# Two cross-attention layers on one core: L0's keys written once to DRAM, and each batch's rows loaded in four transfers

## The reference, cut to what matters

```
q = x @ Wq + bq          # 32 query heads of 16
k = ctx @ Wk + bk        # 8 key heads of 16, each shared by 4 query heads
v = ctx @ Wv + bv
attn = softmax(q k^T / 4 + mask)
x = layernorm((attn v) @ Wo + bo + x)
```

## Time and profile before

| | |
|---|---|
| median of 3 runs | 2464.18 us |
| profiled execution | 2464.88 us, its span 2463.0 us |
| granted TensorE clock, mean | 0.981 |
| moved by DMA | 250.46 MB in 134533 packets |
| SyncE's queue (q1) | 90863 packets, 125.37 MB, 17.0% of 16 engines |
| ScalarE's queue (q10) | 43496 packets, 122.76 MB, 16.2% |

### The profile page before, as it was taken

The page is one execution under the profiler, slowest core; times in us unless marked ns, Lnnn a source line. Parts: engine busy times, 40 slices in busy tenths (PEclk is TensorE's granted clock), DMA queues, the critical chain, the costliest instruction groups (busy, mean ns, idle before and its releaser), DMA issues. The chain is left out here.

```text
span 2463.0 us, 36589 instructions
## 1 busy us (share of the span) xinstructions
PE 2320.6 (94%) x13464; PEld 2087.0 (85%) x13464; DVE 1401.3 (57%) x3146; ACT 999.3 (41%) x2195; POOL 765.6 (31%) x823
## 2 busy tenths in 40 slices
PE   6898899999999999998988979999999999999998
PEld 5666899998989999997876769998989999998976
DVE  4687645454565455456548965455546655454574
ACT  3685433243433333243238944243334333243420
POOL 2132322415141423313531331414141422415055
PEclk9899999999999999999999989999999999999999
DMA  8351323233323323234363213333332323233222
GB/s 279 96 156 39 92 85 108 87 91 116 99 86 96 95 82 111 82 96 146 125 198 96 77 40 95 97 101 97 103 95 82 96 90 107 86 87 121 79 76 79
DMA packets 134533, 250.46 MB, mean 102 GB/s; under 512 B 31151, under 2 KB 54831, under 8 KB 133335
## 3 DMA queue, kind: packets, MB, share of 16 engines
q1 hardware_dynamic: 90863, 125.37, 17.0%
q10 hardware_dynamic: 43496, 122.76, 16.2%
HBM read 223.19 MB, written 29.48 MB: 103 GB/s over the span
## 5 line engine op out<-in xcount | busy, mean ns | idle before, releaser
L674 POOL TENSOR_SCALAR wk_hi<-raw 128x512 fp32r<-128x512 f32 (+1 forms) x84 | 54.0, 643 | 905.5 <-DMA raw<-in_wk 747.5
L1411 ACT ACTIVATE probs<-scores,prm 112x376 f32<-112x376 f32 x256 | 147.1, 575 | 342.9 <-DVE prm L1805 342.8
L794 PE MATMUL pj_two<-ctx_hi,wk_hi 128*128 128x376 f32 x708 | 243.6, 344 | 7.7 <-DVE rr L1566 4.1
L1566 DVE TENSOR_TENSOR rr<-pj_two,rr 128x448 fp32r<-128x448 f32 (+2 forms) x223 | 147.0, 661 | 172.6 <-ACT rr L1177 172.2
L795 PE MATMUL pj_two<-ctx_lo,wk_hi 128*128 128x376 f32 x708 | 239.0, 338 | 0.0
L796 PE MATMUL pj_two<-ctx_hi,wk_lo 128*128 128x376 f32 x708 | 238.5, 337 | 0.0
L794 PE MATMUL pj_two<-pt_hi,nat 125*128 125x448 f32 x531 | 198.8, 374 | 10.6 <-issue 10.2
L676 POOL TENSOR_TENSOR wb_lo<-raw,wb_hi 128x512 fp32r<-128x512 f32 x152 | 197.9, 1302 | 12.7
L1568 DVE SCALAR_TENSOR_TENSOR k_lo<-pj_two,cur,k_hi 128x375 fp32r<-128x375 f32 x167 | 101.3, 607 | 173.1 <-ACT k_hi L1179 172.6
L796 PE MATMUL pj_two<-pt_hi,nat 125*128 125x448 f32 x531 | 195.4, 368 | 0.0
L795 PE MATMUL pj_two<-pt_lo,nat 125*128 125x448 f32 x531 | 195.2, 368 | 0.0
(11 more groups left out here) (278 smaller groups left out, 6611.1 us busy)
## 6 DMA issues: line engine op xcount, KB each, us to landing
nat<-nat_scratch ACTq DMA_DIRECT2D x256, 384.0 KB, 3.7
raw<-in_wq SPq DMA_DIRECT2D x72, 256.0 KB, 3.3
raw<-in_wo SPq DMA_DIRECT2D x72, 256.0 KB, 2.6
raw<-in_wk SPq DMA_DIRECT2D x64, 256.0 KB, 3.8
raw<-in_wv SPq DMA_DIRECT2D x64, 256.0 KB, 4.2
raw<-in_w SPq DMA_DIRECT2D x64, 256.0 KB, 2.9
nat_scratch<-rr ACTq DMA_DIRECT2D x7, 1536.0 KB, 8.8
k_hi<-keys_scratch SPq DMA_DIRECT2D x32, 188.0 KB, 2.8
```

What stands on the lines that cost most here:

```text
L674: nc.gpsimd.tensor_scalar(hi, src, 1.0, 0.0, ALU.mult, ALU.add).then_inc(split_hi, 1)
L794: nc.tensor.matmul(dst, l_hi, r_hi, start=first, stop=False)
L1411: nc.scalar.activation(probs[0:L, h, 0:SK], scores[n % SCR][0:L, 0:SK], ACT.Exp, bias=neg_max[0:L, h:h + 1], accum_out=row_sum[0:L, h:h + ...
L1566: i = nc.vector.tensor_tensor(dst, src, hi.bitcast(F32), ALU.subtract)
```

## The change

The scratch loses its dimension e, so keys are stored once: two transfers a batch in place of four. The second copy is made by the load, which reads each 16 rows twice, by a source whose first dimension has step 0 and count 2. This needs one transfer for each key head and part: four of 32 rows in place of one of 128. The semaphore counts follow.

```diff
--- before.py
+++ after.py
@@ -254,7 +254,7 @@
 
     ctx_dram = nc.dram_tensor("ctx_copy", (D, HB, S), F32, kind="Internal").ap()
 
-    k_dram = nc.dram_tensor("keys0_scratch", (HALVES, HB, 8, 2, 2, HD0, SK), F32, kind="Internal").ap()
+    k_dram = nc.dram_tensor("keys0_scratch", (HALVES, HB, 8, 2, HD0, SK), F32, kind="Internal").ap()
     q_dram = nc.dram_tensor("queries0_scratch", (HALVES, C0, HPC, 2, HD0, T), F32, kind="Internal").ap()
 
     x_dram = nc.dram_tensor("x_copy", (D, B * L), F32, kind="Internal").ap()
@@ -433,21 +433,23 @@
                     load_rows(base + RAW_A + ag * RAW_GU, wk, ag // G1 * D, ag % G1 * GW)
 
                 def store_keys0(b, split, n):
-
                     sp.wait_ge(split, n)
                     for r in range(2):
-                        for e in range(2):
-                            sp.dma_start(k_dram[hf, b, :, r, e, :, :], k0_split[b % 2][r].bitcast(F32)).then_inc(k0_out[b % 2], 16)
+                        sp.dma_start(k_dram[hf, b, :, r, :, :], k0_split[b % 2][r].bitcast(F32)).then_inc(k0_out[b % 2], 16)
 
                 def load_keys0(c, b):
+
                     if c == 0:
-                        sp.wait_ge(k0_out[b % 2], (hf * 2 + b // 2 + 1) * 64)
+                        sp.wait_ge(k0_out[b % 2], (hf * 2 + b // 2 + 1) * 32)
                     else:
 
                         sp.wait_ge(sc_ready, hf * SC_H + (c - 1) * HB * HPC + (b + 1) * HPC)
                     sp.sem_inc(sp_passed, 1)
-                    sp.dma_start(k_hi[:, b, :].bitcast(F32),
-                                 k_dram[hf, b, 2 * c:2 * c + 2].rearrange("g r e d n -> (g r e d) n")).then_inc(k0_in[b], 16)
+                    for kv in range(KV2):
+                        for r in range(2):
+                            at = 64 * kv + 32 * r
+                            sp.dma_start(k_hi[at:at + 32, b, :].bitcast(F32),
+                                         k_dram[hf, b, 2 * c + kv, r].unsqueeze(0).broadcast_to([2, HD0, SK])).then_inc(k0_in[b], 16)
 
                 def store_queries0(c, split, n):
                     sp.wait_ge(split, n)
@@ -921,7 +923,7 @@
                 def scores0(n):
                     c, b, j = n // (HB * HPC), n // HPC % HB, n % HPC
                     if n % HPC == 0:
-                        pe.wait_ge(k0_in[b], (hf * C0 + c + 1) * 16)
+                        pe.wait_ge(k0_in[b], (hf * C0 + c + 1) * 64)
                         if c > 0:
                             pe.wait_ge(q0_in[b], (hf * (C0 - 1) + c) * 64)
                         elif b == 0:
@@ -1292,7 +1294,7 @@
                 def keys0(b, bank, ready, n, mid):
 
                     if hf * 2 + b // 2 > 0:
-                        act.wait_ge(k0_out[b % 2], (hf * 2 + b // 2) * 64)
+                        act.wait_ge(k0_out[b % 2], (hf * 2 + b // 2) * 32)
                     if hf == 0 and b == 0:
                         act.wait_ge(setup_dve, 1)
                     move(k0_split[b % 2][0], bank[:, 0:SK], ready, n, bias=bk0, mid=mid)
@@ -1364,7 +1366,7 @@
                         exps0(n + 3)
                     if n == 20:
                         for t in k0_out:
-                            act.wait_ge(t, (hf + 1) * 2 * 64)
+                            act.wait_ge(t, (hf + 1) * 2 * 32)
                         act.sem_inc(w_free["k"], 1)
                     if n >= 16 and n % 8 == 0:
                         out0((n - 16) // 8)
```

## The result

| | before | after |
|---|---|---|
| median | 2464.72 us (2457.64 to 2472.16, 20 runs) | 2469.14 us (2466.25 to 2472.86, 20 runs) |
| ratio of after to before, 95% interval | | 1.0018 [1.0011, 1.0024] |
| profiled execution, its span | 2464.88, 2463.0 us | 2467.31, 2465.5 us |
| granted clock, mean | 0.981 | 0.981 |

The changed kernel is 4.4 us slower (2.7 to 5.9 by the interval). A second set of 7 runs gave 2469.61 us against 2464.27, ratio 1.0029 [1.0018, 1.0040]: 5.3 us by the medians, 4.4 to 9.9 by the interval. The sign and the range held. The size did not: I had 12.

A forecast was written before the change was run, and what follows sets the result against it. TensorE, busy 94% of the span, was taken as the bound, so only its waits in L0 count. Terms 1.0 + 5.4 + 3.8 + 1.0 + 1.0 = +12.2 us gave 2476 us, range 2463 to 2487.

The forecast's parts named there:

- (a): Half 0 until the queries of c = 0 land: three store batches -6.6, loads of two batches +7.6, sum +1.0 us.
- (b): From queries landed to ScalarE's eviction into pt_hi: loads of batches 2 and 3 +3.8 each, batch 3's stores -2.2, sum +5.4 us.
- (c): Half 0, c = 2, batch 0: 56 more rows on the engine pair delay the load and queries behind by +3.8 us.
- (e): TensorE's longer waits keep the clock low longer: one more low stretch, about +1 us, bounds 0 and +3.
- (d): Half 1 until its last query store lands: three store batches -6.6, loads of batches 0 and 1 +7.6, sum +1.0 us.
- saved stores win: Rival: loads spread over sixteen engines or land early enough, so only the stores' saving counts; 2451 us, chance 0.10.
- They cancel: Rival: engine pairs rotate, or the pair was not late before 59.90 us; +2 us, 2466 us, chance 0.13.
- Late weights too: Rival: in c = 2 weight loads behind four key loads reach GpSimd late, 5 to 10 us more; 2484 us, chance 0.07.
- some query weights reach GpSimd sooner: Sign that the forecast is wrong: query weights reaching GpSimd sooner than before the change.
- landing of key loads: Sign: key loads land after some 6 us and more where they were 2.8; 3 us would be wrong.

The follow-up runs named there:

- loads alone: Keys stored twice as in the kernel before, but loaded by four transfers of 32 rows with the repeat: 2485.97 us, 1.0095 of the kernel before.
- stores alone: Keys stored once, loaded by one transfer of 128 successive rows (partly wrong keys): 2446.32 us, 0.9935 of the kernel before.
- again: The changed kernel, same code, run and profiled a second time: 2469.61 us, 1.0029 of the kernel before.
- eight loads of 16 rows: Changed kernel with each 32-row load split into two of 16 rows without the repeat, eight a batch: 2462.91 us, 0.9996 of the kernel before.
- pair only for c = 0: Changed kernel with repeating loads only for c = 0, one 128-row load (partly wrong keys) for c = 1 to 3: 2468.41 us, 1.0013 of before.

## Why the prediction was right and wrong, step by step

The view that the load would run on two engines, the same two, at some 68 ns a row, and that the ends of L0's starts are set by the stores that ScalarE waits for, was right: shares 0.13 and 0.14, 64 ns. The sizes by step, of the profiled executions:

| step | predicted | measured | loads alone | stores alone |
|---|---|---|---|---|
| (a) to queries in | +1.0 (+7.6, -6.6) | +0.6 (again: +0.6) | +6.5 | -10.3 |
| (b) to pt_hi | +5.4 (+7.6, -2.2) | +4.4 (+3.9) | +6.6 | -0.5 |
| (c) and (e) to the 7th output | +4.8 | +2.5 (+2.1) | +2.7 | -0.5 |
| (d) half 1 to L0's last output | +1.0 (+7.6, -6.6) | -0.8 (-0.3) | +7.4 | -8.6 |

"7th output" is the seventh of L0's outputs in half 0 that GpSimd scales, at 148.57 before and 156.13 after; half 1 is counted from ScalarE's store of half 0's outputs (1254.84 before, 1258.78 after) to the last of L0's outputs (1433.77 and 1436.88). The kernel before, profiled again, lies within 0.8 us of the first in each of steps (a) to (c), 1.8 us below it in their sum, and 1.7 us above it in (d).

**(a)** was right as a sum, by luck. Its terms were +7.6 and -6.6; alone they are worth +6.5 and -10.3, and together +0.6, not -3.8. The pair that the loads fill eats the saving of the stores on the same engines: 6.99 us for the issue of two stores.

**(b)** came out 1.0 us below. From the queries to the start of batch 3's load it is 15.63 us in place of 14.80: +0.8 where batch 2's load and batch 3's stores were to make +1.6. From there to pt_hi it is 9.70 in place of 6.09: +3.6, where I had +3.8 of rows. I had counted the three further issues of a batch at nothing, and here SyncE spends 2.2 us more on them (2.54 us in place of 0.36). But they lie beside the rows: from 78.5 us on the pair works without a pause (33 rows in 1 us), its tail ends at some 85.5 us, and 56 rows at 64 ns are 3.6 us by themselves. That the issues add to it isn't shown. The eight loads of 16 rows, with no narrow source, lose 2.3 us in this step, which I put down to their issues (3.55 us a batch).

**(c)** is the step that failed in half 0: "so 56 more rows on the pair, and the queries behind them, are late by +3.8 us". The wait grew by 1.7 us (2.9 to 4.6; in the second profiles 2.1 and 4.4), and 3.6 us of it remain with a wide load in c = 2. The kernel with the pair only for c = 0 gives narrow loads in c = 1 to 3 a price of 1 us in all. It isn't that the copies come late: SyncE issues them 45.5 us after pt_hi in the kernel before, 45.4 in the changed one, and 45.5 with the pair only for c = 0. The step took the engines to be free for a wide load when the copies end. But in the kernel before they are still full as TensorE's wait ends at 145.31 (share 1.14; columns as in the earlier trace rows), where in the changed kernel two of sixteen work from 147 to 150 us:

```profile
145.00:146.00 1.00, 0.69 (x5) 0.70 (x6) 0.25 (x1) 0.00 (x0) 0.00 (x0) 1.00 1.14 259
```

So a wide load's rows run among others that the narrow one's lack, which would make the difference less than 56 rows. That this makes up the missing 2 us is a reading that no run tests, and why the wait with wide loads comes out anywhere from 2.1 to 3.6 us stays open. **(e)** was right: TensorE's 10 us after the wait hold 52 matmuls where they held 60, and at 37 in 5 us these 8 are 1.1 us. The clock's row:

```profile
151.50:156.50 5.00, 4.64 (x19) 3.60 (x20) 2.75 (x9) 1.72 (x3) 0.37 (x1) 0.50 0.37 98
```

**(d)** is the other: +1.0 forecast, -0.3 to -0.8 measured against the first profile of the kernel before, -2.0 to -2.5 against the second. The stores' term, -6.6, was too small: alone they give -8.6 by the first profile and -10.3 by the second. The loads' term, +7.6, was right or too large: +7.4 and +5.7. The rival "saved stores win" had capped it at the wait of 4.7 us, but the query weight's wait (3.7 us) is behind the same queue and falls with it.

Half 0 was to cost 11.2 us and cost 7.6 by the 7th output; half 1 was to cost 1.0 and gave 0.8 back. That leaves +6.7 us in L0 by this profile (+6.3 by the second), and the spans differ by 2.5. The missing 4.2 us lie in the wide attentions and the MLP, which the change doesn't touch. From L0's last output of half 0 to the store of half 0's outputs the twelve profiled executions, of all kernels, took 1029.4 to 1037.3 us, and the two of the changed kernel 1030.5 and 1036.7 (before: 1034.2 and 1036.2). Where TensorE's clock falls there differs from one execution to the next: from 1150 to 1174 us its mean was 0.72 in the profile before and 0.93 in the one after. Single executions can't settle 2 or 3 us. The medians say +4.4 and +5.3, the second interval reaches to +9.9, and whether L0's +6.5 is given back in part elsewhere or these are chance isn't settled.

**The rivals.** "Saved stores win" needed loads under 1 us of extra landing: refuted, though its 13 us were too small for a kernel where that holds (stores alone: 18). "They cancel" (2466) came nearest in size, with the wrong mechanism: no pair rotates, and (b) came nearly in full. "Late weights too" (2484) didn't happen: GpSimd's waits for query weights from 15 to 80 us fell from 40.4 to 37.5 us, and its first split came at 37.3 in place of 41.7 us, the second at 56.2 in place of 49.9. That some query weights reach GpSimd sooner was one of my signs for "wrong"; it shows how far the stores' gain reached, but TensorE's wait for weights stayed at 8.2 us. Of the landing of key loads, a sign I had named, the profile after gives no number.

In one sentence: I set the loads at +27 us and the stores at -15, they are worth +22 and -18, and the error of each, small against itself, is large against the difference.

## What to carry to other kernels

Read how many DMA engines a transfer has from the share while it runs alone (0.13 is two, 0.50 eight), and give both sides an outermost count like those that ran wide here (16, 32, 64 or 128 rows at one step): a layout of the scratch that makes all stores and loads wide gave 25 us here, with the keys stored once or twice, where halving the bytes and reading them through a repeat lost 4 to 5. When a change removes rows from busy engines and adds rows to some of them, measure each side alone before adding up; the two here were -18 and +22 us. And a DMA issue, 0.3 to 0.6 us here, can count where its ring isn't full: loads in eight pieces had no narrow source, and gained 1 us where the load in one piece gained 18.

## What the runs showed of the hardware

Issue times depend on the shape. An issue on SyncE's queue took 0.35 us for the load of 128x376, 0.44 us for one of 16x376 without a repeat, 0.55 for 64x376 to every second partition (1.10 for two; 0.60 in the median of all 64), and 0.59 us in the median for 2x16x376 with a repeat:

```profile
L451 SPq DMA_DIRECT2D k_hi<-keys_scratch x128: 575/586/4227, 34.0 to 1405.4; - x128
```

The longest, 4.2 us, stood behind a full ring. A load to every second partition isn't narrow: while a batch's loads are alone, from 63.25 to 64 us in that kernel, SyncE's queue keeps 53% of sixteen engines busy on average. By the page of that kernel (part 6) it landed after a median 2.4 us, where the load of 128 rows took 2.8.

```profile
q1 hardware_dynamic: 82, 0.10, 53.0%
```
```profile
k_hi<-keys_scratch SPq DMA_DIRECT2D x64, 94.0 KB, 2.4
```
